# Graph attention: constant rows added by matmuls over 128 partitions instead of 4

## The chip, the cores and the metric

The kernel runs on one core of one Trainium2 chip. The metric is the device time of one execution in microseconds (us), taken as the median of several runs. Of this kernel, changes of under 0.2% (about 6.4 us) can hardly be told from no change.

## The reference, cut to what matters

A conditioned transformer layer (`L0`) is followed by a graph attention layer (`L1`) over the same rows. There are 2 batches of 2048 rows with 512 features each, 16 heads of 32, and 20 graph nodes (the first rows of each batch) that every row attends to, in two directions.

```python
def reference(x, cond, mask, ...):
    x = L0(x, cond, ...)                 # adaptive norm, attention, adaptive norm, MLP
    v, q, adj_f = x, cond, mask.astype(float32)
    row_zero = v.sum(-1) == 0
    q_exp = where(row_zero[..., None], 0.0, q[:, None, :])
    self_feat = concatenate([v, q_exp], -1) @ W_self.T + b_self
    output = self_feat
    for d in range(2):
        A = (adj_f if d == 0 else swapaxes(adj_f, 1, 2))[:, :, :20, :]
        cond_adj, vb = A.sum(-1), A @ w_bias + b_bias
        kv = self_feat[:, :20]
        qh, kh = heads(self_feat @ Wq[d].T + bq[d]), heads(kv @ Wk[d].T + bk[d])
        aff = einsum('bnhd,bmhd->bnhm', qh, kh) / sqrt(32)
        w = softmax(where(cond_adj[:, :, None] > 0, aff, -9e15) + vb[:, :, None])
        output = output + out_heads(w, kv, Wout[d]) + bout[d]
    return v + relu(output)
```

For a row `x` of the graph layer, both the scores of all heads and the `self_feat` part are linear in `x`, plus a part that depends only on whether the row's sum is zero (then the condition vector drops out), plus constants. These last two parts are what the change is about.

## The kernel before, in words

The kernel is one program in which each engine has its own instruction list, written out by hand; semaphores order the lists against each other. The stages are: projections, attention, output projection, feed-forward (eight chunks of 512 rows, 16 slices of the hidden layer each), a shared stage that folds the graph weights, and the graph stage over 32 tiles of 128 rows.

TensorE (`pe` in the code, PE in the profile; its weight loads are PEld) does each matmul as a weight load, up to 128 rows by 128 columns, and a stream of up to 512 columns through these weights. Most operands are rounded float32 (`F32R`) in high and low halves, three products for one.

In the graph stage a tile `t` takes these steps on TensorE, in this order of lines in the profile:

- `pe_score(t + 1)`: 24 matmuls of 320 columns at L1728 (two directions into two PSUM banks), then two at L1732 that add the constant rows: the weights are `nzT`, four rows by 128 columns, and the stream is `rows`, four rows by 320 columns.
- `pe_turn_w(t)`: six transposes at L1753 of the softmax weights `ex`; `pe_turn_x(t + 2)`: four transposes at L1711 of the next rows.
- `pe_self(t + 1)`: 12 matmuls of 512 columns at L1741, then one at L1743 that adds the constant rows of this part, four rows again.
- `pe_turn_nz(t + 2)`: one transpose at L1718 that turns `nzt` (128 rows by 4 columns: twice "the row's sum isn't zero", twice 1) into PSUM, from where ScalarE copies it into `nzT` (L1803).
- `pe_heads(t)`: six products at L1762, in 12 matmuls, of the turned weights `wT` with `vw`.

Beside it VectorE adds the edge bias (L1877), takes maxima, sums and reciprocals of the softmax and writes the output (L1898); GpSimd (POOL) subtracts the maximum (L1928) and multiplies by the reciprocal (L1931); ScalarE does the exponential and copies.

`rows` has four rows for each batch: the condition's part in high and low half, and the constant part in high and low half. They are written once by VectorE in `dve_rows` (L1341), twice in the last feed-forward chunk and four times in the shared stage. `pool_graph_start(1)` fills four tiles with zeros in the last feed-forward chunk (L1424 to L1427). `pool_graph` fills `nzt` with ones before the tiles (L1922).

Of the kernel before, what the change touches and what calls it, by code (L numbers as in the profile page):

```python
# [7 lines left out]
F32 = mybir.dt.float32  # L8
F32R = mybir.dt.float32r
I32 = mybir.dt.int32  # L10
ALU = mybir.AluOpType
ACT = mybir.ActivationFunctionType
AX = mybir.AxisListType

B, S, D = 2, 2048, 512
# [163 lines left out]
def program(nc, a):  # L179
    pe, act, dve, pool, sp = nc.tensor, nc.scalar, nc.vector, nc.gpsimd, nc.sync  # L180
# [14 lines left out]
    with ExitStack() as ctx:  # L195
        cursor = [(nc.sbuf_base + 31) // 32 * 32]

        def sem(name):
            return ctx.enter_context(nc.semaphore(name))

        def place(name, shape, at, dt=F32):
            return nc.alloc_sbuf_tensor_at(name, list(shape), dt, offset=at)

        def take(name, shape, dt=F32):
            at = cursor[0]
            cursor[0] += (4 * int(np.prod(shape[1:])) + 31) // 32 * 32
            return place(name, shape, at, dt)

        ps = ctx.enter_context(nc.psum_tensor("ps", [128, 8, 512], F32))
# [926 lines left out]
        def early(name, *shape, dt=F32):  # L1136
            n = (4 * int(np.prod(shape[1:])) + 31) // 32 * 32
            if spot[0] < spots[0][1] < spot[0] + n:
                spot[0] = spots[0][1]
            at = spot[0]  # L1140
            spot[0] += n
            at = spots[0][0] + at if at < spots[0][1] else spots[1][0] + at - spots[0][1]
            return place(name, shape, at, dt)[(slice(None),) * len(shape)]

        rt = early("rt", 4, 2, D)
        rows = early("rows", 4, B, D + 640, dt=F32R)
        brow, bm = early("brow", 3, D), early("bm", 120, 96)
        wbB, m4, sel, onb = early("wbB", 128, 12), early("m4", 128, 4), early("sel", 4, 2), early("onb", 3, 4)
        colb, condT2 = early("colb", 128, 5, NK), early("condT2", 128, NK, B)
# [8 lines left out]
               (0, 1): place("gm01", [128, NK, 320], at1 + 54272), (1, 1): place("gm11", [128, NK, 320], at1 + 59392)}  # L1158
        s_cw_wc, s_cw_wv, s_cw_k0, s_cw_q0, s_cw_k1, s_cw_q1, s_cw_nat, s_cw_o0 = s_qst
        n_cw = 32 * NC8 + 16  # L1160
        s_cw_o1, s_small, s_x40 = sem("s_cw_o1"), sem("s_small"), sem("s_x40")
        (s_xT, s_xTc, s_nz, s_nzm, s_nzb, s_prep, s_qt, s_qtc, s_kvm, s_kv, s_rowm, s_rhi,
         s_rlo, s_khm, s_kh, s_gmm, s_gma, s_gmd, s_ggm, s_ggh, s_ggl, s_vwm, s_vw, s_wvh, s_wvl) = (
            sem(n) for n in ("s_xT", "s_xTc", "s_nz", "s_nzm", "s_nzb", "s_prep",
# [168 lines left out]
        def dve_rows(i, b, bank, c0, w):  # L1333

            hi, lo = rt[:, 0, 0:w], rt[:, 1, 0:w]
            dve.wait_ge(s_rhi, i + 1)
            dve.tensor_tensor(lo, ps[0:4, bank, 0:w], hi, ALU.subtract).then_inc(s_rlo, 1)
            dve.wait_ge(s_rlo, 3 * i + 1)
            dve.tensor_scalar(lo, lo, sel[:, 1:2], None, ALU.mult).then_inc(s_rlo, 1)
            dve.wait_ge(s_rlo, 3 * i + 2)  # L1340
            dve.scalar_tensor_tensor(out=rows[:, b, c0:c0 + w], in0=hi, scalar=sel[:, 0:1], in1=lo, op0=ALU.mult,  # L1341
                                     op1=ALU.add).then_inc(s_rlo, 1)

        def dve_kh(d, bank):
# [76 lines left out]
        def pool_graph_start(f):  # L1421

            if f == 1:
                pool.memset(lc[:, :, :, 2:4], 0.0).then_inc(s_prep, 1)  # L1424
                pool.memset(lq, 0.0).then_inc(s_prep, 1)
                pool.memset(lb[:, :, :, 0:2], 0.0).then_inc(s_prep, 1)
                pool.memset(kvr.rearrange("p d b k h e n -> p (d b k h e n)"), 0.0).then_inc(s_prep, 1)  # L1427
            elif f == 2:
                pool.wait_ge(s_small, 16 * NSMALL)
                pool.tensor_copy(lc[:, :, :, 0:2], condT2.rearrange("p k b -> p b k").unsqueeze(3)  # L1430
                                 .to_broadcast([128, B, NK, 2])).then_inc(s_prep, 1)
                pool.tensor_copy(lb[:, :, :, 2:4], colb[:, 1:3, :].unsqueeze(3)
                                 .to_broadcast([128, 2, NK, 2])).then_inc(s_prep, 1)
            elif f == 6:
                kvT4 = kvT.rearrange("p k (b n) -> p k b n", b=B)
                pool.wait_ge(s_kv, 3)
                pool.wait_ge(s_prep, 4)
                for b in range(B):
                    for d in range(2):
                        pool.tensor_copy(kvr[:, d, b, :, :, d, :], kvT4[:, :, b, :].unsqueeze(2)  # L1440
                                         .to_broadcast([128, NK, 3, NG])).then_inc(s_prep, 1)
                pool.tensor_copy(lq[:, :, :, 0:2], qtT.rearrange("p k b -> p b k").unsqueeze(3)
                                 .to_broadcast([128, B, NK, 2])).then_inc(s_prep, 1)
                pool.wait_ge(s_prep, 11)
                for b in range(B):
                    pool.tensor_copy(lq[:, b, :, 2:4], colb[:, 0, :].unsqueeze(2)
                                     .to_broadcast([128, NK, 2])).then_inc(s_prep, 1)
# [79 lines left out]
        def ff_over(eng):  # L1527

            eng.wait_ge(s_f1, NQ)
            eng.wait_ge(s_f2, 4 * NQ)  # L1530
            eng.wait_ge(s_ro, 4 * NC8)
# [132 lines left out]
        rc = take("rc", [128, 2, 32])  # L1664
        tsum = take("tsum", [128, 2])
        nzt = take("nzt", [128, 2, 4])
        nzT = take("nzT", [4, 2, 128], F32R)
        s_xt, n_xt = s_x3, [(NT - 1 - i) // 5 + 1 for i in range(5)]
        s_ad, n_ad = s_a3, [(NT - 1 - i) // 3 + 1 for i in range(3)]
        s_st, n_st = s_x2, [(NT - 1 - i) // 5 + 1 for i in range(5)]  # L1670
# [6 lines left out]
        def weights_read(eng):  # L1677

            eng.wait_ge(s_gmm, 16)
            for t in range(4):  # L1680
                eng.wait_ge(s_rs[t], 16 * (n_rs + NC8))
# [117 lines left out]
        def act_turn_nz(t):  # L1799
            act.wait_ge(s_tz, t + 1)  # L1800
            if t >= 2:
                act.wait_ge(s_self, t - 1)
            act.activation(nzT[:, t % 2, :], ps[0:4, 7, 0:128], ACT.Copy).then_inc(s_zT, 1)  # L1803

        def act_turn_w(t):
            for r0, q0, q1 in ((120, 0, 3), (120, 3, 4), (80, 4, 6)):
# [27 lines left out]
        def dve_zero(t):  # L1834
            j = t % 2
            dve.wait_ge(s_zs, t + 1)
            dve.wait_ge(s_nz1, 1)
            if t >= 2:
                dve.wait_ge(s_tz, t - 1)
            dve.tensor_scalar(nzt[:, j, 0:2], tsum[:, j:j + 1].to_broadcast([128, 2]), 0.0, None,  # L1840
                              ALU.not_equal).then_inc(s_nzv, 1)
# [77 lines left out]
        def pool_graph():  # L1919
            ff_over(pool)  # L1920
            weights_read(pool)
            pool.memset(nzt[:, :, :], 1.0).then_inc(s_nz1, 1)  # L1922
            pool.wait_ge(s_wvl, 1)
            for t in range(NT):
                j = t % 2
                a3, e3 = groups(af[:, j, :]), groups(ex[:, j, :])
                pool.wait_ge(s_mx, t + 1)
                pool.tensor_tensor(a3, a3, mx[:, j, :].unsqueeze(2).to_broadcast([128, 32, NG]),  # L1928
                                   ALU.subtract).then_inc(s_sub, 1)
                pool.wait_ge(s_rc, t + 1)  # L1930
                pool.tensor_tensor(e3, e3, rc[:, j, :].unsqueeze(2).to_broadcast([128, 32, NG]),  # L1931
                                   ALU.mult).then_inc(s_w, 1)
# [83 lines left out]
```

## Time and profile before

| what | us |
|---|---|
| median of 3 runs (3178.0 to 3180.33) | 3179.2 |
| the profiled execution | 3179.57 |
| its span, first to last instruction | 3178.2 |
| TensorE busy in the span | 3132.2 (99%) |
| VectorE busy | 2153.4 (68%) |
| GpSimd busy | 1539.2 (48%) |
| ScalarE busy | 1388.3 (44%) |

The profiled execution is 0.37 us above the median of the runs, and its span is 1.37 us shorter than its time. The graph stage, from the first transposes at 2848 us to the end, is 330 us of the span. In the profile, `4*128` in a matmul's row means weights of four rows by 128 columns; the shape behind it is that of the stream. A matmul's length includes its way through the array, so successive matmuls overlap in the record; the distance between two starts tells how long one holds the engine. Idle time "issue" means that the profile shows nothing that the engine waited for.

### The profile page before, as it was taken

The page shows a single profiled execution, that of the slowest core. Times are in us where ns is not written, and L with a number is a line of the kernel's source. Part 1 is how long each engine was busy: PE and PEld are TensorE (multiplying, and loading weights), DVE is VectorE, ACT ScalarE, POOL GpSimd, SP SyncE. Part 2 cuts the span into 40 slices and gives each one's busy share as a digit, 9 for nine tenths or more (in the row PEclk, how much of TensorE's full clock was granted, in tenths as well). Part 3 has the DMA queues.
Part 4 walks back from the last instruction along what each step waited for, and adds up shares of the span by engine and source line. Part 5 has one row for each costly group of instructions (what it writes and reads, how often), then busy time and mean ns, then how long its engine had stood idle before and what let it go on. Part 6 is the DMA issues. An engine that isn't in the chain of part 4 may idle for free.

```text
span 3178.2 us, 43496 instructions
## 1 busy us (share of the span) xinstructions
PE 3132.2 (99%) x16394; PEld 2171.5 (68%) x16394; DVE 2153.4 (68%) x3633; ACT 1388.3 (44%) x2703; POOL 1539.2 (48%) x654
## 2 busy tenths in 40 slices
PE   8999999999999999999999998999999999999999
PEld 7887655555555555555555546788888887878888
DVE  4557889999999999998998966433333332236666
ACT  2221467666666667666666652311111111113232
POOL 0000488988889889889889854100000001002222
PEclk9999999999999999999999999999999999899999
DMA  6674777978888887878878667311110013112221
GB/s 203 189 234 143 179 166 166 199 151 182 181 174 172 174 184 161 194 169 169 193 153 185 141 167 266 123 40 40 40 40 27 14 40 107 55 32 67 77 77 55
DMA packets 169367, 423.43 MB, mean 133 GB/s; under 512 B 18492, under 2 KB 60604, under 8 KB 141863
## 3 DMA queue, kind: packets, MB, share of 16 engines
q0 software_dynamic: 27744, 201.08, 31.2%
q1 hardware_dynamic: 139639, 214.07, 22.3%
q10 hardware_dynamic: 1776, 5.51, 0.7%
q8 instruction: 130, 2.13, 0.3%
q14 instruction: 78, 0.64, 0.1%
HBM read 143.51 MB, written 75.50 MB: 69 GB/s over the span
## 4 chain that ended last, share of the span: by engine, by line
PE 94%; DVE 2%; DMA 2%; issue 1%; POOL 1%; ACT 1%; SPq 0%; DVEq 0%; ACTq 0%; POOLq 0%
PE ps L384 16%; PE ps L672 15%; PE ps L683 15%; PE ps L1194 11%; PE ps L1181 11%; PE ps L460 5%; PE ps L1728 4%; PE ps L464 3%; PE ps L1741 3%; PE ps L689 2%; PE ps L1762 1%; PE ps L1557 1%; PE ps L1045 1%; DMA ao<-ao_d 1%; PE ps L158 1%; PE ps L1753 1%
## 5 line engine op out<-in xcount | busy, mean ns | idle before, releaser
L397 DVE TENSOR_REDUCE nmp<-ps 128x1 f32<-128x512 f32 x1966 | 1200.1, 681 | 108.2 <-PE ps L384 103.8
L762 ACT ACTIVATE pt<-ps 128x512 f32<-128x512 f32 x2048 | 1030.9, 628 | 458.1 <-PE ps L672 454.8
L861 POOL TENSOR_TENSOR pt<-pt 128x2048 f32<-128x2048 f32 x217 | 995.6, 4588 | 120.2 <-ACT pt L762 114.7
L672 PE MATMUL ps<-qs,ks 128*128 128x512 f32 x2048 | 811.2, 400 | 2.5 <-ACT pt L762 2.5
L384 PE MATMUL ps<-ks,qs 96*128 96x512 f32 x1966 | 804.5, 409 | 0.1
L384 PEld LDWEIGHTS ps<-ks,qs 96*128 96x128 f32 x1966 | 373.3, 190 | 264.5 <-DVE nmp L397 167.0
L683 PE MATMUL ps<-pt,vq 128*32 128x512 f32 x4096 | 492.5, 599 | 0.0
L672 PEld LDWEIGHTS ps<-qs,ks 128*128 128x128 f32 x2048 | 389.9, 191 | 95.5 <-ACT pt L762 18.9
L1181 PE MATMUL ps<-hpb,w 128*128 128x512 f32 x1536 | 384.0, 400 | 3.4 <-DMA x_d<-x 3.4
L1194 PE MATMUL ps<-w,gp 128*128 128x512 f32 x1536 | 379.0, 396 | 1.3 <-DVE gp L1330 1.3
L1181 PEld LDWEIGHTS ps<-hpb,w 128*128 128x128 f32 x1536 | 291.0, 191 | 69.8 <-issue 5.6
L1194 PEld LDWEIGHTS ps<-w,gp 128*128 128x128 f32 x1536 | 288.9, 188 | 69.8 <-DVE gp L1330 1.7
L1328 DVE CAST gp<-g 128x512 fp32r<-128x512 f32 x128 | 60.9, 476 | 400.6 <-ACT g L1317 400.6
L1317 ACT ACTIVATE g<-ps,b1c 128x512 f32<-128x512 f32 x128 | 88.1, 688 | 530.1 <-PE ps L1181 530.1
L1455 POOL TENSOR_TENSOR res<-res,b2B 128x512 f32<-128x512 f32 x32 | 41.3, 1318 | 491.0 <-DMA res<-x_d 491.0
L683 PEld LDWEIGHTS ps<-pt,vq 128*32 128x32 f32 x4096 | 107.2, 109 | 244.7 <-ACT pt L762 163.0
L139 POOL TENSOR_SCALAR ve<-mv 128x4 f32<-128x4 f32 x16 | 4.0, 250 | 383.1 <-DVE mv L134 383.1
L853 POOL DMA_DIRECT2D pt<-pt x189 | 165.8, 877 | 42.3 <-PE ps L683 36.8
L866 POOL TENSOR_TENSOR pt<-pt 128x2048 f32<-128x2048 f32 x31 | 142.6, 4601 | 7.8 <-DMA pt<-pt 3.2
L493 ACT ACTIVATE st<-ps,bqk 128x512 fp32r<-128x512 f32 x64 | 43.8, 688 | 227.1 <-PE ps L460 223.3
L1928 POOL TENSOR_TENSOR af<-af,mx 128x640 f32<-128x640 f32 x32 | 40.8, 1275 | 191.1 <-DVE mx L1883 191.1
L1728 PE MATMUL ps<-gg,xp 128*128 128x320 f32 x768 | 122.7, 317 | 0.0
(169 smaller groups left out, 3020.1 us busy)
## 6 DMA issues: line engine op xcount, KB each, us to landing
pt<-pt POOLq DMA_DIRECT2D x189, 1024.0 KB, 8.5
qk_d<-st SPq DMA_DIRECT2D x128, 256.0 KB, 2.9
qs<-qk_d SPq DMA_DIRECT2D x87, 256.0 KB, 4.8
ks<-qk_d SPq DMA_DIRECT2D x42, 512.0 KB, 8.3
xina<-in_x SPq DMA_DIRECT2D x8, 1024.0 KB, 6.5
v_d<-vst SPq DMA_DIRECT2D x32, 256.0 KB, 2.6
vq<-v_d SPq DMA_DIRECT2D x32, 256.0 KB, 4.3
ao_d<-accs SPq DMA_DIRECT2D x32, 256.0 KB, 6.8
```

Source lines behind the costliest of these rows:

```text
L384: pe.matmul(ps[:, ring.bank["max", u], :], qsb[0:96, v % 3, hq // 4, 128 * (hq % 4):128 * (hq % 4) + 128], ksb[w % 2][0:96, hq // 4, CH * ...
L397: dve.tensor_reduce(nmp[:, n // 4, n % 4:n % 4 + 1], ps[:, ring.bank["max", u], :], AX.X, ALU.max, negate=True).then_inc(s_mr, 1)
L460: m = pe.matmul(ps[:, bank, :], w[:, x, k, col:col + 128], hp[:, y, k, :], start=(i == 0 and k == 0), stop=(i == 2 and k == NK - 1))
L672: pe.matmul(ps[:, score_bank(n), :], ksb[w % 2][:, hh, 128 * kt:128 * kt + 128], qsb[:, v % 3, hh, :], start=True, stop=True).then_inc(s_s ...
L683: m = pe.matmul(ps[32 * hh:32 * hh + 32, 7, :], vq[:, kt, 32 * hh:32 * hh + 32], pt[:, exp_slot(g), hh, :], start=(kt == 0), stop=(kt == 15))
L762: act.activation(pt[:, exp_slot(g), hh, :], ps[:, score_bank(n), :], ACT.Exp, scale=SCALE).then_inc(s_exp, 1)
L853: pool.dma_start(accumulator(v, 1 + d), pt[:, exp_slot(g), :, :], accum_op=ALU.add).then_inc(s_dma[d], 16)
L861: pool.tensor_tensor(accumulator(v, 0), accumulator(v, 0), pt[:, exp_slot(g), :, :], ALU.add).then_inc(s_add, 1)
L866: pool.tensor_tensor(accumulator(v, 0), accumulator(v, 0), accumulator(v, 2), ALU.add).then_inc(s_add, 1)
L1181: m = pe.matmul(ps[:, 4 + r, :], w1[:, f // 4, x, k, 128 * (f % 4):128 * (f % 4) + 128], hp[:, y, k, :], start=(i == 0 and k == 0), stop=( ...
L1194: m = pe.matmul(ps[:, t, :], gp[:, q % 2, x, 128 * t:128 * t + 128], w2[:, f // 4, y, f % 4, :], start=(i == 0 and f == 0), stop=(i == 2 a ...
L1728: pe.matmul(ps[:, 1 + d, 0:320], xp[:, j, x, 128 * k:128 * k + 128], gg[b][:, y, k, 320 * d:320 * d + 320], start=(i == 0 and k == 0), sto ...
```

## The change

`rows` and `nzT` get 128 partitions instead of 4. The four live rows stay in partitions 0 to 3; GpSimd fills both tiles with zeros beforehand, and VectorE (through the new semaphore `s_rz` and one more count of `s_nz1`) waits for these fills before it writes into `rows`, and before the first `nzt`. The matmuls at L1732 and L1743 use all of both tiles. The bytes that a tile takes in a partition are the same.

```diff
-        rows = early("rows", 4, B, D + 640, dt=F32R)
+        rows = early("rows", 128, B, D + 640, dt=F32R)
...
+            dve.wait_ge(s_rz, 1)
+            dve.scalar_tensor_tensor(out=rows[0:4, b, c0:c0 + w], in0=hi, scalar=sel[:, 0:1], in1=lo, op0=ALU.mult,
...
             if f == 1:
+                pool.memset(rows.rearrange("p b n -> p (b n)").bitcast(F32), 0.0).then_inc(s_rz, 1)
                 pool.memset(lc[:, :, :, 2:4], 0.0).then_inc(s_prep, 1)
...
-        nzT = take("nzT", [4, 2, 128], F32R)
+        nzT = take("nzT", [128, 2, 128], F32R)
...
-            act.activation(nzT[:, t % 2, :], ps[0:4, 7, 0:128], ACT.Copy).then_inc(s_zT, 1)
+            act.activation(nzT[0:4, t % 2, :], ps[0:4, 7, 0:128], ACT.Copy).then_inc(s_zT, 1)
...
-            dve.wait_ge(s_nz1, 1)
+            dve.wait_ge(s_nz1, 2)
...
             weights_read(pool)
+            pool.memset(nzT[:, :, :].rearrange("p t n -> p (t n)").bitcast(F32), 0.0).then_inc(s_nz1, 1)
             pool.memset(nzt[:, :, :], 1.0).then_inc(s_nz1, 1)
```

TensorE's, ScalarE's and SyncE's lists keep their order; each matmul stands where it stood. GpSimd's list gets two rows. Before, in the last feed-forward chunk and up to the first tile of the graph stage (`kvr`, `lc`, `lq`, `lb` are operands of the shared stage):

```order
547 L1424 MEMSET lc 128x8x2 [waits s_lo]
548 L1425 MEMSET lq 128x32
549 L1426 MEMSET lb 128x8x2
550 L1427 MEMSET kvr 128x1920
551 L1430 COPY lc<-condT_120 128x8x2 [waits s_small]
```

After, at the same place, then at the start of the graph stage:

```order
547 L1425 MEMSET rows 128x2304 [waits s_lo]
548 L1426 MEMSET lc 128x8x2
549 L1427 MEMSET lq 128x32
550 L1428 MEMSET lb 128x8x2
551 L1429 MEMSET kvr 128x1920
552 L1432 COPY lc<-condT_120 128x8x2 [waits s_small]
...
559 L1924 MEMSET nzT 128x256 [waits s_vst0,s_vst1,s_gmm,s_vst2,s_ro,s_vst3,s_f2,s_f1]
560 L1925 MEMSET nzt 128x8
561 L1931 TENSOR_TENSOR af<-af,mx 128x640 [waits s_mx,s_wvl]
```

The fill of `rows` now stands ahead of the four older fills, and the fill of `nzT` ahead of that of `nzt`; what follows on GpSimd comes in the same order as before. Line numbers behind the new lines move by one to three.

## Rows read from the trace of the kernel before

**Rows 1.** Busy time by stretch: stretch, PE, PEld, DVE, ACT, POOL busy, granted clock, DMA

```profile
2900.00:2950.00 50.00, 50.00 (x312) 42.81 (x310) 34.90 (x67) 15.17 (x41) 12.74 (x10) 1.00 0.23 76
```

**Rows 2.** Chain of waits, 2780 to the end: start, length, what

```profile
2945.72 0.48 PE ps L1732 x2
...
3165.43 0.50 PE ps L1732 x2
...
3175.43 0.69 DVE ot L1898
```

**Rows 3.** TensorE, 2940.16 to 2940.72: start, length, what, rows*columns of its weights, shape

```profile
2939.85 0.39 PE L1741 MATMUL ps<-wvp,xp 128*128 128x512 f32 x1
2940.17 0.50 PE L1743 MATMUL ps<-rows,nzT 4*128 4x512 f32 x1
2940.60 0.27 PE L1718 MATMUL ps<-ident,nzt 128*4 128x128 f32 x1
```

**Rows 4.** TensorE inside a run of L1741

```profile
2939.16 1.08 PE L1741 MATMUL ps<-wvp,xp 128*128 128x512 f32 x4
```

**Rows 5.** TensorE around L1732's two matmuls, from four windows in order of time

```profile
2944.98 0.75 PE L1728 MATMUL ps<-gg,xp 128*128 128x320 f32 x4
...
2945.42 0.31 PE L1728 MATMUL ps<-gg,xp 128*128 128x320 f32 x1
2945.66 0.41 PE L1732 MATMUL ps<-rows,nzT 4*128 4x320 f32 x1
...
2945.91 0.30 PE L1732 MATMUL ps<-rows,nzT 4*128 4x320 f32 x1
...
2946.14 0.87 PE L1753 MATMUL ps<-ident,ex 128*120 128x128 f32 x6
2946.85 0.60 PE L1711 MATMUL ps<-ident,xt 128*128 128x128 f32 x4
```

**Rows 6.** Line L1743: its weight loads (ns min/median/max), and idle before them (us, times)

```profile
L1743 PEld LDWEIGHTS ps<-rows,nzT x32: 181/182/182, 2861.6 to 3169.4; 4*128 4x128 f32 x32
...
  issue: 11.4, 32
```

**Rows 7.** Line L1728: weight loads of all 128 rows (ns min/median/max)

```profile
L1728 PEld LDWEIGHTS ps<-gg,xp x768: 187/188/337, 2852.1 to 3165.0; 128*128 128x128 f32 x192
```

**Rows 8.** TensorE elsewhere: a full-row transpose right behind 512-column matmuls

```profile
2590.86 0.40 PE L1194 MATMUL ps<-w,gp 128*128 128x512 f32 x1
2591.09 0.27 PE L158 MATMUL ps<-ident,xinb 128*128 128x128 f32 x1
```

**Rows 9.** TensorE elsewhere: a matmul with four weight columns behind 512-column matmuls

```profile
2696.41 0.40 PE L1194 MATMUL ps<-w,gp 128*128 128x512 f32 x1
2696.73 0.59 PE L1251 MATMUL ps<-wcT,lc 128*4 128x512 f32 x1
```

**Rows 10.** TensorE at the first tile: the four-column transpose behind L1711

```profile
2848.32 0.66 PE L1711 MATMUL ps<-ident,xt 128*128 128x128 f32 x4 [0.31 <-DVE vw L1640]
2848.81 0.27 PE L1718 MATMUL ps<-ident,nzt 128*4 128x128 f32 x1
```

**Rows 11.** In order of time: last feed-forward chunk, then GpSimd's fill in the shared stage

```profile
2657.73 1.70 POOL L1427 MEMSET kvr<- 128x1920 f32 x1
...
2658.87 0.84 DVE L1328 CAST gp<-g 128x512 fp32r<-128x512 f32 x1 [3.49 <-ACT g L1317]
...
2663.54 2.96 PE L1194 MATMUL ps<-w,gp 128*128 128x512 f32 x12
...
2781.62 0.10 POOL L1922 MEMSET nzt<- 128x8 f32 x1 [90.15 <-PE ps L1211]
```

**Rows 12.** Line L1840 on VectorE (ns min/median/max)

```profile
L1840 DVE TENSOR_SCALAR nzt<-tsum x32: 159/1089/1093, 2848.3 to 3158.0; 128x2 f32<-128x2 f32 x32
```

**Rows 13.** GpSimd and TensorE one tile on, in order of time

```profile
2953.14 1.28 POOL L1931 TENSOR_TENSOR ex<-ex,rc 128x640 f32<-128x640 f32 x1 [3.80 <-DVE rc L1892]
...
2956.13 0.87 PE L1753 MATMUL ps<-ident,ex 128*120 128x128 f32 x6
```

More of the change, by code:

```diff
@@ L1160, in program @@
         n_cw = 32 * NC8 + 16
-        s_cw_o1, s_small, s_x40 = sem("s_cw_o1"), sem("s_small"), sem("s_x40")
+        s_cw_o1, s_small, s_x40, s_rz = sem("s_cw_o1"), sem("s_small"), sem("s_x40"), sem("s_rz")
         (s_xT, s_xTc, s_nz, s_nzm, s_nzb, s_prep, s_qt, s_qtc, s_kvm, s_kv, s_rowm, s_rhi,
@@ L1340, in dve_rows @@
             dve.wait_ge(s_rlo, 3 * i + 2)
-            dve.scalar_tensor_tensor(out=rows[:, b, c0:c0 + w], in0=hi, scalar=sel[:, 0:1], in1=lo, op0=ALU.mult,
+            dve.wait_ge(s_rz, 1)
+            dve.scalar_tensor_tensor(out=rows[0:4, b, c0:c0 + w], in0=hi, scalar=sel[:, 0:1], in1=lo, op0=ALU.mult,
                                      op1=ALU.add).then_inc(s_rlo, 1)
```

## The prediction

> **What bounds the kernel now.** I read the busy time by stretch first. In the graph stage TensorE is busy for all of the 50 us that are shown, at a granted clock of 1.00 (the upper level, 2.4 GHz), while VectorE has 34.9, GpSimd 12.7 and ScalarE 15.2 us of work [rows 1]. The chain of waits says the same: tile after tile it runs through TensorE alone, and leaves it only behind the last L1732 at 3165.43, for a tail through the other engines that ends with the last output at 3175.43 + 0.69 us [rows 2]. So whatever holds TensorE in a tile counts 30 times, once a lap of 2956.13 - 2946.14 = 9.99 us [rows 5, 13].
>
> Then I read TensorE's starts in order of time, since successive matmuls overlap in the record and only distances between starts tell what one costs. A plain L1741 of 512 columns takes (1.08 - 0.39) / 3 = 0.23 us to the next start [rows 4]; a plain L1728 of 320 columns (0.75 - 0.31) / 3 = 0.147; a plain transpose L1711 (0.60 - 0.27) / 3 = 0.11 [rows 5]. The four-row matmuls cost more on both of their sides, though they stream no more columns. L1741 to L1743 takes 0.32 us, and L1743 to the next start 0.43, both against 0.23 [rows 3]. L1728 to the first L1732 takes 0.24, the first to the second 0.25, the second to L1753 0.23, all against 0.147, and the six L1753 that follow have (0.87 - 0.27) = 0.60 us between their first and last start instead of 5 x 0.11 = 0.55 [rows 5].
>
> Why they cost more shows in the weight loads. The load for L1743 is preceded by 11.4 us of idle time in 32 times, 0.36 us each, and ends it for no reason that the profile has a name for [rows 6]. No semaphore stands ahead of L1743, so this isn't data that came late. A full 128-row load takes 0.188 us [rows 7], more than the 0.147 from one L1728 to the next, so full-row loads do lie beside the stream before them. The four-row load of 0.182 us doesn't: engine and weights are emptied before it, and again before the full-row load after it.
>
> **The change part by part.** L1743 and L1732 become matmuls of the very form of L1741 and L1728: the same rows, columns, type and stream length. I take their distances as the plain ones. What each place gives back in a tile:
>
> - ahead of L1743: 0.32 - 0.23 = 0.09 us
> - behind L1743: 0.43 - 0.23 = 0.20 us
> - ahead of the first L1732: 0.24 - 0.147 = 0.093 us
> - between the two: 0.25 - 0.147 = 0.103 us
> - behind the second: 0.23 - 0.147 = 0.083 us
> - in the L1753 behind it: 0.60 - 0.55 = 0.05 us
>
> Together 0.62 us of the lap of 9.99. The counts differ. The tail begins at the last L1732, so the two at L1743 count for 31 tiles, those up to the second L1732 for 32, those behind it for the 30 tiles in which L1753 follows and which aren't the last. The sum is 31 x 0.29 + 32 x 0.196 + 30 x 0.133 = 8.99 + 6.27 + 3.99 = 19.25 us. Each distance is rounded to 0.01 us, so this can be off by some 2 us.
>
> The 0.20 is the term to doubt, because what follows L1743 is L1718, a transpose with weights of only four columns. Two rows bound it. A full transpose behind a 512-column matmul starts after 2591.09 - 2590.86 = 0.23 us, no penalty [rows 8]. An ordinary matmul with four weight columns starts after 2696.73 - 2696.41 = 0.32 us, 0.09 more [rows 9]. L1718 itself is seen behind L1711 once at the upper clock: the last of the four L1711 starts at 2848.32 + 0.66 - 0.27 = 2848.71, and L1718 0.10 later, the plain distance of transposes [rows 10]. A transpose with four columns pays nothing there, so I take 0.23 and keep 0.32 as the other end. The Trainium skill (TensorEngine Tiling, Overview and Tiling Modes) has small column counts run in a narrower tiling mode and the engine drained whenever the mode changes; by this L1718 would keep a drain and the sum be 16.5. Its restrictions (Tile-to-Partition Mapping) say that column tiling goes without transposes of fp32 input; by this L1718 runs in the full array, and the sum stays 19.25. The row of L1718 agrees with the second.
>
> The new 128-row loads take 0.188 us instead of 0.182 [rows 6, 7] and lie beside the stream ahead of them, as those of L1728 do. If that cover were gone, each would stand in the open, and the result is the rival of no gain, below.
>
> The fills are GpSimd's. That of `rows` is estimated from the 128x1920 fill: 1.70 x 2304 / 1920 = 2.04 us [rows 11]. It goes ahead of this fill in the last feed-forward chunk, so the work queued behind it, four fills and some copies, comes about 2 us later. GpSimd's work and VectorE's can collide: the cast L1328 beside that fill took 0.84 us [rows 11], and L1840 takes 0.159 us alone but 1.09 as its usual case, while GpSimd is at L1928 [rows 12]. If both fills held the cast to their end, it would begin at 2657.73 + 1.70 + 2.04 = 2661.47, be over by 2662.31 and leave 1.23 us for L1330, which works on a tile of the same size (0.84 us, by estimate, at the length of that cast), before TensorE's next L1194 at 2663.54 [rows 11]. So a cover of about 0.4 us is left in the worst case; I cost the fill at nothing, and at 1 us if the cover is gone. VectorE needs `s_rz` first behind slice 7 of the chunk, and the fill is issued by slice 2; a slice is 24 matmuls of 0.23 us, 5.5 us, so there are over 25 us between. The fill of `nzT`, 1.70 x 256 / 1920 = 0.23 us, stands ahead of the fill of `nzt` at 2781.62 [rows 11], which VectorE's first L1840 needs at 2848.3 [rows 12]: 66 us of cover. Each `dve_rows` now waits for one more semaphore, which has long been raised. Nothing else moves.
>
> What is late next: the softmax chain from L1732 over VectorE, GpSimd, ScalarE and back to L1753. It begins at the second L1732, 2945.91 [rows 5], GpSimd's L1931 ends at 2953.14 + 1.28 = 2954.42, and TensorE takes it up at 2956.13 [rows 13]: 1.71 us to spare. A lap shorter by 0.62 leaves 1.09. VectorE has 34.9 / 50 x 9.99 = 7.0 us of work in a lap [rows 1] that will be 9.37. So TensorE stays the bound.
>
> **The sum** is 3179.57 - 19.25 = 3160.3 us for the profiled execution, which is 0.37 above the median of the runs; for the median I predict 3160.0 us, 0.6% less.
>
> **The rivals.**
>
> *The transpose keeps its stall.* 0.09 x 31 = 2.8 us less of a gain: 3162.8 us. For it speaks the 0.32 of rows 9, against it the 0.10 of rows 10. Chance 10%.
>
> *The rows are not what costs.* The gaps could belong to these accumulating matmuls, to their tiles or to their place, and stay with 128 rows: 3179.2 us, as before. For it: in the graph stage no matmul but these two has four rows, so rows and place aren't told apart there. Against it: loads of the same columns and type are beside the stream everywhere else. The Trainium skill (TensorE: Matmul & The Clock Gate, "Why this matters for your kernels") says that a single matmul of 32 rows takes as long as one of 128, and (Part 3) that a load passes a running matmul only where it goes to other rows of the array; by these rules filling up rows gains nothing. The loads of rows 7, longer than the distance between their matmuls, don't agree with the second. Chance 6%.
>
> *Only a part comes.* If one of the two lines keeps its stalls, the gain is 8.99 or 10.26 us: 3170.2 or 3168.9 us. Nothing in the rows speaks for that. Chance 2%.
>
> *Slower: the shorter lap sets GpSimd against VectorE.* Each collision such as L1840's adds 1.09 - 0.16 = 0.93 us [rows 12] to the chain that ends at L1753. Up to 1.71 us it costs no more than the gain; beyond this the lap is longer than before. Three new collisions are 2.79 us, 1.08 over the point: 30 x 1.08 = 32 us, 3212 us. Against it: almost all of the chain hangs on L1732 itself and moves with it as a whole, and only L1898, which waits for L1762, shifts within it. Chance 2%.
>
> **How the numbers follow.** The forecast has 80%. Its own spread is the rounding (2 us) and that of the runs (1.2 us): 3157 to 3163. The range reaches over the transpose's case with the same spread, 3157 to 3166, and leaves out the rest. Faster by more than 0.2%, below 3172.8, are the forecast, the transpose's case and the partial one: 92%. Within 0.2%, which is what a measurement here can't tell from no change: 6%. Slower: 2%.
>
> **What would show it.** In the profile after, L1732 and L1743 should read `128*128`; L1741 to L1743 and L1743 to L1718 should take 0.23 us, the four distances at L1732 0.147; the idle time "issue" ahead of the loads of L1732 and L1743 should be gone and that ahead of L1753 too; the lap should be 9.37 us, and VectorE's wait ahead of L1877 shorter by 0.6. An L1718 at 0.32 shows the transpose's case. Idle time of TensorE ahead of L1753 with GpSimd as its releaser, in mid-stage, shows the last rival. Distances of 0.32 and 0.43 with 128 rows would make the prediction wrong at its root.

## The result: 3156.7 us, 0.7% faster, and the profile after

| what | before | after |
|---|---|---|
| median of 6 runs each, us | 3178.6 (3169.32 to 3184.61) | 3156.66 (3143.74 to 3160.59) |
| ratio after/before, 95% interval | | 0.9929 [0.9905, 0.9952] |
| the profiled execution, us | 3179.57 | 3160.59 |
| lap of the graph stage, start to start of the 24 score matmuls, median, us | 9.987 | 9.327 |

The kernel got faster by the mechanism that was predicted. The time lies 3.3 us under the forecast of 3160.0 and 0.34 us under the low end of its range. In the profile of after the line numbers of the graph stage are two to three higher (L1728, L1732, L1741, L1743, L1718, L1753 became L1730, L1734, L1743, L1745, L1720, L1755).

The first part of the page of after, the busy time of each engine in the span:

```profile
span 3159.2 us, 43504 instructions
...
PE 3110.9 (98%) x16394; PEld 2172.3 (69%) x16394; DVE 2157.3 (68%) x3633; ACT 1388.7 (44%) x2703; POOL 1542.9 (49%) x656
```

TensorE lost 21.3 us of the 3132.2 before, and the span 19.0. VectorE and GpSimd gained 4 us each, which cost nothing. Where the time came from shows in the weight loads. This is L1745 of after, the line that was L1743 [rows 6], with its weight loads (ns min/median/max, first and last start):

```profile
L1745 PEld LDWEIGHTS ps<-rows,nzT x32: 187/188/188, 2862.9 to 3150.2; 128*128 128x128 f32 x32
```

There is no row "issue" any more: the 11.4 us of idle time that no semaphore explained are gone. From the first load to the last it is 287.3 us; in [rows 6] it was 307.8. These 20.5 us, over 31 laps, are the change. The span lost 1.5 us less: in this profile the first transposes of the graph stage start 3.2 us later, at 2851.51 us against 2848.32 in [rows 10], and 1.7 of them were made good ahead of the first and behind the last of these loads.

One lap of after in order of time, from four windows (start, length, what), to be held against [rows 3, 5, 13]:

```profile
2950.73 0.31 PE L1730 MATMUL ps<-gg,xp 128*128 128x320 f32 x1
2950.88 0.46 PE L1734 MATMUL ps<-rows,nzT 128*128 128x320 f32 x2
...
2951.18 0.82 PE L1755 MATMUL ps<-ident,ex 128*120 128x128 f32 x6
2951.38 0.89 DVE L1879 TENSOR_TENSOR af<-ps,c 128x320 f32<-128x320 f32 x2 [1.96 <-PE ps L1734]
...
2953.27 1.23 DVE L1842 TENSOR_SCALAR nzt<-tsum 128x2 f32<-128x2 f32 x1
...
2954.79 0.39 PE L1743 MATMUL ps<-wvp,xp 128*128 128x512 f32 x1
2955.02 0.39 PE L1745 MATMUL ps<-rows,nzT 128*128 128x512 f32 x1
2955.24 0.27 PE L1720 MATMUL ps<-ident,nzt 128*4 128x128 f32 x1
...
2958.27 1.28 POOL L1934 TENSOR_TENSOR ex<-ex,rc 128x640 f32<-128x640 f32 x1 [3.80 <-DVE rc L1894]
...
2960.50 0.82 PE L1755 MATMUL ps<-ident,ex 128*120 128x128 f32 x6
```

Read the distances of starts. L1743 to L1745 takes 0.23 us, where [rows 3] had 0.32; L1745 to the transpose L1720 0.22, where it was 0.43. L1730 to the first L1734 takes 0.15, the two L1734 are 0.46 - 0.31 = 0.15 apart, and the second is 0.15 ahead of L1755; in [rows 5] these were 0.24, 0.25 and 0.23. The six L1755 lie 0.82 - 0.27 = 0.55 apart, no longer 0.60. The lap is 2960.50 - 2951.18 = 9.32 us, that of [rows 5, 13] 9.99. GpSimd's L1934 ends at 2959.55, 0.95 us ahead of the L1755 that needs it: the softmax chain became tighter by 0.76 us, and still doesn't bound. TensorE is as full as in [rows 1], with more in the same stretch:

```profile
2900.00:2950.00 50.00, 50.00 (x336) 46.76 (x336) 38.25 (x72) 15.11 (x40) 13.83 (x11) 1.00 0.23 76
```

It issues 336 matmuls in 50 us instead of 312. That VectorE went from 34.9 to 38.25 us is mostly more laps in the stretch (34.9 x 9.987 / 9.327 = 37.4). The rest fits L1842, the L1840 of [rows 12]: it takes 1.23 us a lap now instead of 1.09, off the path.

The fills held up VectorE longer than GpSimd's fills did before, and still cost nothing. GpSimd, VectorE and TensorE of after in the last feed-forward chunk, then GpSimd's fill in the shared stage (the engines' other rows between these are left out):

```profile
2662.06 2.02 POOL L1425 MEMSET rows<- 128x2304 f32 x1
...
2663.70 2.44 DVE L1328 CAST gp<-g 128x512 fp32r<-128x512 f32 x1 [3.49 <-ACT g L1317]
...
2664.17 1.69 POOL L1429 MEMSET kvr<- 128x1920 f32 x1
2665.82 0.38 POOL L1432 COPY lc<-condT 128x16 f32<-128x16 f32 x1
...
2666.18 0.70 DVE L1330 TENSOR_TENSOR gp<-g,gp 128x512 fp32r<-128x512 f32 x1
2668.37 2.96 PE L1194 MATMUL ps<-w,gp 128*128 128x512 f32 x12
2669.29 0.43 DVE L1328 CAST gp<-g 128x512 fp32r<-128x512 f32 x1 [2.42 <-ACT g L1317]
...
2786.14 0.31 POOL L1924 MEMSET nzT<- 128x256 f32 x1 [90.22 <-PE ps L1211]
```

The cast began in the fill of `rows` and ended at 2666.14, when GpSimd was done with both long fills and about done with the copy behind them: 2.44 us, against 0.84 in [rows 11] and 0.43 for the next cast, which has no fill beside it. L1330 was done at 2666.88, and TensorE's next L1194 came at 2668.37: 1.5 us to spare.

### The profile page after: what moved, and what is told of

Read it like the earlier page. It is cut to its first block, busy times and chain, and to the rows that moved or that the text cites. A ratio compares the mean times of both kernels' runs of the same rounds, so it can differ in the third digit from the quotient of the medians.

```text
span 3159.2 us, 43504 instructions
## 1 busy us (share of the span) xinstructions
PE 3110.9 (98%) x16394; PEld 2172.3 (69%) x16394; DVE 2157.3 (68%) x3633; ACT 1388.7 (44%) x2703; POOL 1542.9 (49%) x656
## 4 chain that ended last, share of the span: by engine, by line
PE 94%; DVE 2%; DMA 2%; issue 1%; POOL 1%; ACT 1%; SPq 0%; DVEq 0%; ACTq 0%; POOLq 0%
PE ps L384 16%; PE ps L672 15%; PE ps L683 15%; PE ps L1194 11%; PE ps L1181 11%; PE ps L460 5%; PE ps L1730 4%; PE ps L464 3%; PE ps L1743 3%; PE ps L689 2%; PE ps L1764 1%; PE ps L1559 1%; PE ps L1045 1%; DMA ao<-ao_d 1%; PE ps L158 1%
## 5 line engine op out<-in xcount | busy, mean ns | idle before, releaser
L672 PE MATMUL ps<-qs,ks 128*128 128x512 f32 x2048 | 810.5, 399 | 2.5 <-ACT pt L762 2.5
L672 PEld LDWEIGHTS ps<-qs,ks 128*128 128x128 f32 x2048 | 389.1, 190 | 95.4 <-ACT pt L762 18.9
L1181 PE MATMUL ps<-hpb,w 128*128 128x512 f32 x1536 | 381.9, 398 | 3.4 <-DMA x_d<-x 3.4
L1194 PE MATMUL ps<-w,gp 128*128 128x512 f32 x1536 | 380.4, 396 | 2.1 <-DVE gp L1330 2.1
L1194 PEld LDWEIGHTS ps<-w,gp 128*128 128x128 f32 x1536 | 289.4, 188 | 71.4 <-DVE gp L1330 2.5
L1181 PEld LDWEIGHTS ps<-hpb,w 128*128 128x128 f32 x1536 | 289.0, 190 | 69.8 <-issue 5.6
L1730 PE MATMUL ps<-gg,xp 128*128 128x320 f32 x768 | 121.7, 315 | 0.0
```

Source lines behind the costliest of these rows:

```text
L672: pe.matmul(ps[:, score_bank(n), :], ksb[w % 2][:, hh, 128 * kt:128 * kt + 128], qsb[:, v % 3, hh, :], start=True, stop=True).then_inc(s_s ...
L1181: m = pe.matmul(ps[:, 4 + r, :], w1[:, f // 4, x, k, 128 * (f % 4):128 * (f % 4) + 128], hp[:, y, k, :], start=(i == 0 and k == 0), stop=( ...
L1194: m = pe.matmul(ps[:, t, :], gp[:, q % 2, x, 128 * t:128 * t + 128], w2[:, f // 4, y, f % 4, :], start=(i == 0 and f == 0), stop=(i == 2 a ...
L1730: pe.matmul(ps[:, 1 + d, 0:320], xp[:, j, x, 128 * k:128 * k + 128], gg[b][:, y, k, 320 * d:320 * d + 320], start=(i == 0 and k == 0), sto ...
```

## The experiments

The lap below is the median distance, over the whole graph stage, from the start of one tile's score matmuls to that of the next; it repeats to some ns between profiles, while the medians of runs move by several us (a part of the reason is shown further down). No kernel here leaves any of the computation out. Where no median of several runs is given, the kernel ran once.

**The fills alone.** After, with both matmuls reading four rows again.

```diff
-                pe.matmul(ps[:, 1 + d, 0:320], nzT[:, j, :], rows[:, b, D + 320 * d:D + 320 * d + 320],
+                pe.matmul(ps[:, 1 + d, 0:320], nzT[0:4, j, :], rows[0:4, b, D + 320 * d:D + 320 * d + 320],
...
-            pe.matmul(ps[:, 3 + j, :], nzT[:, j, :], rows[:, b, 0:D], start=False, stop=False,
+            pe.matmul(ps[:, 3 + j, :], nzT[0:4, j, :], rows[0:4, b, 0:D], start=False, stop=False,
```

> Both tiles have 128 partitions and both fills run, but the matmuls at L1734 and L1745 read partitions 0 to 3 only. Theory A (what costs is that a matmul with four rows stands between matmuls with 128: the engine empties on both sides): a lap of 9.99 us as in the kernel before, starts 0.32 and 0.43 us apart around L1745, a median within 3 us of the kernel before. Theory B (the place of the tiles, or the wait for the fills, brought the gain): a lap near 9.33 us and about 20 us less than before. If the fills cost something it shows here alone, as up to 1 us more.

Measured: 3182.41 us, ratio to before 0.9999 [0.9984, 1.0014], lap 9.987. Its L1745:

```profile
L1745 PEld LDWEIGHTS ps<-rows,nzT x32: 181/181/181, 2863.9 to 3171.7; 4*128 4x128 f32 x32
...
  issue: 11.4, 32
```

The idle time is back to the digit. So the larger tiles, the fills and the added waits leave the lap as it was and change the time by nothing that these runs can tell; the gain is in the rows that the matmuls read.

**One line each.** After, with L1745 alone on four rows (the score part is kept), and with L1734 alone on four rows (the self part is kept): one of the two edits above each.

> L1734 reads 128 partitions, L1745 only 0 to 3. Theory A with independent places: a lap of 9.99 - 0.093 - 0.103 - 0.083 - 0.05 = 9.66 us, about 10.3 us less than before. Theory C (one four-row matmul in a lap is enough to hold the engine, so either half alone brings little): a lap over 9.8 us. The starts at L1745 keep 0.32 and 0.43 us.

> L1745 reads 128 partitions, L1734 only 0 to 3. Theory A: a lap of 9.99 - 0.09 - 0.20 = 9.70 us by rounded starts, about 9 us less than before. If the pace inside L1743 (0.232 us before, 0.227 at its end after) is also set by L1745, the lap is 9.65 us. Theory C: over 9.8 us.

Measured, score part: lap 9.640, 0.347 less than before; 3166.65 us, 0.9957 [0.9941, 0.9972]. Self part: lap 9.693, 0.294 less; 3174.79 us, 0.9975 [0.9964, 0.9986]. Each line pays for itself, and the two together (0.641) make 0.660 but for 0.02. This 0.02 is in the pace of the 12 full-row matmuls of `pe_self` (L1743, before L1741): the eleven distances between their starts, by the medians over the laps, sum to 2.636 us in the kernel before and with the self part, 2.628 with the score part, and 2.607 with both. L1745 with the score part, then with the self part:

```profile
L1745 PEld LDWEIGHTS ps<-rows,nzT x32: 181/181/182, 2849.3 to 3146.3; 4*128 4x128 f32 x32
```

```profile
L1745 PEld LDWEIGHTS ps<-rows,nzT x32: 187/188/188, 2862.0 to 3160.5; 128*128 128x128 f32 x32
```

From the first load to the last these are 297.0 and 298.5 us, 10.8 and 9.3 less than the 307.8 of [rows 6]. By the laps the parts are worth 31 x 0.347 = 10.8 and 31 x 0.294 = 9.1 us; by the medians, 16.0 and 7.9 (before in the same call: 3182.65). The medians aren't good enough to divide 20 us into two parts; that of the score part rests on four runs, one of them 10 us below the next. That run is the profiled one, and it is taken up below.

**After once more,** the same kernel beside those three.

> The changed kernel once more, for the size. Theory A: the laps give 31 x 0.66 = 20.5 us, so a ratio of 0.9935 with an interval that holds it, and single runs spread over some 10 us because of stages before the graph stage. Theory D (the change also gains elsewhere, such as in the feed-forward or the shared stage): a ratio below 0.992 and a shorter stretch before the first transposes of the graph stage than the 2848.3 us of before, beyond what single profiles differ by.

Measured: 3158.72 us (3153.59 to 3165.31), 0.9927 [0.9914, 0.994], lap 9.327 again. The two medians of after are 2 us apart.

**How many rows.** After, with both matmuls on 64, 65 or 33 rows of the same tiles:

```diff
...
-            pe.matmul(ps[:, 3 + j, :], nzT[:, j, :], rows[:, b, 0:D], start=False, stop=False,
+            pe.matmul(ps[:, 3 + j, :], nzT[0:64, j, :], rows[0:64, b, 0:D], start=False, stop=False,
...
```

> The matmuls at L1734 and L1745 read partitions 0 to 63, zeros from 4 on. Theory A1 (the array is split by rows in steps, and up to 64 rows go into a split array, which must be emptied before and after): a lap of 9.99 us, 0.32 and 0.43 us around L1745 as with four rows. Theory A2 (cost falls with every row added): 60 of 124 rows added, a lap of about 9.67 us. Theory A3 (only very few rows cost): 9.33 us.

> As before this with partitions 0 to 64. Theory A1: 65 rows no longer fit the half array and run as full ones, so a lap of 9.33 us, 0.227 us on both sides of L1745. Theory A2: 9.66 us, next to that of 64 rows. If only a full set of 128 rows is free of the stall: 9.99 us.

> As before this with partitions 0 to 32. Theory A1: a split array again, 9.99 us. Theory A2: 9.83 us. Theory A3: 9.33 us.

Measured: 64 rows 3181.96 us, lap 9.98; 65 rows 3158.16 us, lap 9.353; 33 rows 3187.49 us, lap 9.98 (before in that call: 3182.22). L1745 with 64 rows, with 65, and with 33, one fence each:

```profile
L1745 PEld LDWEIGHTS ps<-rows,nzT x32: 182/183/183, 2863.2 to 3170.9; 64*128 64x128 f32 x32
...
  issue: 11.3, 32
```

```profile
L1745 PEld LDWEIGHTS ps<-rows,nzT x32: 187/188/188, 2858.4 to 3146.5; 65*128 65x128 f32 x32
```

```profile
L1745 PEld LDWEIGHTS ps<-rows,nzT x32: 182/183/183, 2869.2 to 3176.8; 33*128 33x128 f32 x32
...
  issue: 11.3, 32
```

One row more, from 64 to 65, takes the whole stall away, and the load's time steps with it from 183 to 188 ns; 33 and 64 rows stall just as four do. So it isn't a cost that grows or shrinks with the rows, but a state with a border between 64 and 65. The Trainium skill (TensorEngine Tiling (Array Packing), Tiling Modes) has 32-row, 64-row and 128-row modes, and an engine that is drained when the mode changes. The traces agree with a border behind 64 rows, with a lap of 9.98 us on the one side and 9.353 on the other; of the drain they show the idle time ahead of the loads, 11.3 us or none, and between 4 and 33 rows they show no border. That a matmul changes sides by its rows alone, with nothing else in the program changed, is this measurement's.

**Four-row matmuls side by side.** Before, with the four-row matmul of the self part moved right behind the two of the score part, so that the tile leaves the full-row work once instead of twice. It opens the sum in its bank instead of closing it, and waits for the bank.

```diff
+            if t >= 2:
+                pe.wait_ge(s_out, t - 1)
+            pe.matmul(ps[:, 3 + j, :], nzT[:, j, :], rows[:, b, 0:D], start=True, stop=False, skip_group_check=True)
...
-                              start=(i == 0 and k == 0), stop=False, skip_group_check=True)
-            pe.matmul(ps[:, 3 + j, :], nzT[:, j, :], rows[:, b, 0:D], start=False, stop=False,
-                      skip_group_check=True).then_inc(s_self, 1)
...
+                              start=False, stop=False, skip_group_check=True)
+            m.then_inc(s_self, 1)
```

> The kernel before, with four rows; but the four-row matmul of the self part is issued right behind the two at L1732, opens its PSUM bank, and the 12 of L1741 add to it. Theory A (the array is emptied where the row mode changes): two changes of mode in a lap instead of four. The 0.09 ahead of the matmul goes, of the 0.20 behind it about 0.1 goes (the emptying) and 0.1 stays (its load in the open, as between the two L1732): a lap of 9.80 us, about 6 us less than before. Theory E (each four-row matmul has a price of its own wherever it stands): a lap of 9.99 us and no difference.

Measured: 3172.4 us, 0.9973 [0.9957, 0.9989], lap 9.70. TensorE of it at the place, in order of time:

```profile
2910.29 0.56 PE L1732 MATMUL ps<-rows,nzT 4*128 4x320 f32 x2
2910.69 0.39 PE L1736 MATMUL ps<-rows,nzT 4*128 4x512 f32 x1
2911.01 0.32 PE L1755 MATMUL ps<-ident,ex 128*120 128x128 f32 x1
```

The second L1732 starts at 2910.29 + 0.25 = 2910.54 and L1736 0.15 behind it: among four-row matmuls the plain distance holds, and the load doesn't stand in the open. The 0.32 behind L1736 is one return to full rows. So the price is one for each change between few rows and full rows, not one for each four-row matmul. The 0.25 between the two L1732 belongs to the change as well: it is the second start after it, and the third, L1736, is on time.

**One change more.** Before, with the self part's matmul cut into two of 256 columns, the first among the 12 full-row ones.

```diff
+                    if (i, k) == (1, 1):
+                        pe.matmul(ps[:, 3 + j, 0:256], nzT[:, j, :], rows[:, b, 0:256], start=False, stop=False,
+                                  skip_group_check=True)
-            pe.matmul(ps[:, 3 + j, :], nzT[:, j, :], rows[:, b, 0:D], start=False, stop=False,
+            pe.matmul(ps[:, 3 + j, 256:512], nzT[:, j, :], rows[:, b, 256:512], start=False, stop=False,
```

> The kernel before, with the four-row matmul L1743 cut into two of 256 columns: one behind the sixth of the 12 matmuls of L1741, one where it stood. The same columns are streamed, but a lap has six changes between four-row and full-row weights instead of four. Theory A (the change of mode is paid, whatever is streamed): the 0.09 ahead and the 0.20 behind are paid once more, a lap of 9.99 + 0.29 = 10.28 us, some 9 us more than before. Theory E (the four-row stream itself is slow, by the column): a lap of 9.99 us.

Measured: 3193.95 us (before 3181.42), lap 10.387, 0.400 more. TensorE at the place:

```profile
2911.81 1.32 PE L1741 MATMUL ps<-wvp,xp 128*128 128x512 f32 x5
2913.05 0.38 PE L1744 MATMUL ps<-rows,nzT 4*128 4x256 f32 x1
2913.36 0.50 PE L1741 MATMUL ps<-wvp,xp 128*128 128x512 f32 x1
```

The last of the five L1741 starts at 2911.81 + 1.32 - 0.39 = 2912.74, L1744 0.31 later, and the next L1741 0.31 behind that. With the same columns streamed in all, one more time out of the full rows and back costs 0.40 us a lap. Both distances of 0.31 are a part of it, and by the medians of the starts the second L1741 after the return comes 0.337 us behind the first, where the same place takes 0.231 in the kernel before. So the return makes two starts late here. Behind L1718 it doesn't: L1762 follows it after 0.108 us before as after (L1764 behind L1720). Read like this, the 0.43 behind L1743 in [rows 3] holds two late starts at once, the second after the way in and the first after the way out; that reading wasn't tested by itself.

**The same for columns.** In the shared stage of after, two kinds of matmul have weights of four columns. Here they get 68 (the further ones zero or unused).

```diff
-        lc, lq, lb = early("lc", 128, B, NK, 4), early("lq", 128, B, NK, 4), early("lb", 128, 2, NK, 4)
+        lc, lqb = early("lc", 128, B, NK, 4), early("lqb", 128, 2, NK, 72)
+        lq, lb = lqb[:, :, :, 0:68], lqb[:, :, :, 4:72]
...
-                pe.matmul(ps[0:4, i, 0:320], lq[:, b, k, :], gm_[d, b][:, k, :], start=(k == 0), stop=False,
+                pe.matmul(ps[0:68, i, 0:320], lq[:, b, k, :], gm_[d, b][:, k, :], start=(k == 0), stop=False,
```

> The changed kernel, and in the shared stage the weights of the two matmul groups with four columns (lq and lb) are widened to 68 columns with zeros, or in four of them with other rows' values that nobody reads. Theory A for columns (over 64 columns the array is not split): L1559 to L1568 takes 0.269 us instead of 0.362, L1571 to L1600 0.07 instead of 0.162, and the next one 0.105 instead of 0.180: 4 x 0.26 = 1.0 us less in the shared stage, too little for the median, which stays within 3 us of the changed kernel's. If narrow columns are not what costs there: 0.362 and 0.162 as before.

Measured: 3158.6 us, 0.992 [0.9894, 0.9946], lap 9.327. The first of these matmuls in after, and then here:

```profile
2794.68 0.70 PE L1559 MATMUL ps<-gm,wnat 128*128 128x320 f32 x2
2795.31 0.43 PE L1568 MATMUL ps<-gm,lq 128*4 128x320 f32 x1
```

```profile
2792.97 0.43 PE L1562 MATMUL ps<-gm,wnat 128*128 128x320 f32 x1
2793.24 0.43 PE L1571 MATMUL ps<-gm,lqb 128*68 128x320 f32 x1
```

With four columns the distance is 2795.31 - (2794.68 + 0.70 - 0.43) = 0.36 us, with 68 it is 0.27, and so it is in all four places of the stage: narrow weights among full ones pay the 0.09 of [rows 9] too. It happens too seldom here to be seen in the time of the kernel.

**The clock in the shared stage.** Why did one run of the score part take 10 us less than the next? TensorE of before in the shared stage, and the stretch around it (busy time of PE, PEld, DVE, ACT, POOL; granted clock; DMA), each in a fence of its own, and then the same two views of that run:

```profile
2757.57 3.74 PE L1203 MATMUL ps<-kvT,wkT 128*128 128x40 f32 x32 [0.94 <-PE ps L1194]
2761.13 20.20 PE L1211 MATMUL ps<-khb,wqn 128*128 128x80 f32 x96
```

```profile
2760.00:2785.00 25.00, 25.00 (x116) 23.63 (x116) 5.44 (x10) 4.42 (x7) 0.10 (x1) 0.53 0.10 30
```

```profile
2758.33 3.74 PE L1203 MATMUL ps<-kvT,wkT 128*128 128x40 f32 x32 [0.94 <-PE ps L1194]
2761.89 10.92 PE L1211 MATMUL ps<-khb,wqn 128*128 128x80 f32 x96
```

```profile
2760.00:2785.00 25.00, 25.00 (x170) 20.59 (x170) 8.38 (x15) 6.56 (x12) 0.35 (x2) 1.00 0.21 70
```

The same 96 matmuls take 20.20 us at the lower level of the clock (1.2 GHz) and 10.92 us at the upper one (2.4 GHz): 9.3 us between two executions, on lines that the change doesn't touch. In after they take:

```profile
2765.10 20.75 PE L1211 MATMUL ps<-khb,wqn 128*128 128x80 f32 x96
```

Of the profiles with these 80 columns, eleven have 19.9 to 20.8 us here, and this one 10.92. What goes ahead of the fall is L1203, 32 matmuls of 40 columns, each behind a load of 128 rows; the same 32, in the same 3.74 us, go ahead in the score part's run, in which no fall follows, and why is not shown. To see whether the fall hangs on how short the streams are, the last experiment but one doubles the columns of the 96 (160 in three of four, the further 80 overwritten by the next matmul):

```diff
+            kf = khb[:, d, b, :, :].rearrange("p g n -> p (g n)")
...
-                m = pe.matmul(ps[:, bank, 80 * g:80 * g + 80], wqn[d][:, g, 128 * kin:128 * kin + 128],
-                              khb[:, d, b, g, :], start=True, stop=True)
+                n = 160 if g < NK - 1 else 80
+                m = pe.matmul(ps[:, bank, 80 * g:80 * g + n], wqn[d][:, g, 128 * kin:128 * kin + 128],
+                              kf[:, 80 * g:80 * g + n], start=True, stop=True)
```

> On the spread of the runs, which the range of the prediction missed. The changed kernel; the matmuls of pe_gm at L1211 stream 160 columns instead of 80 in three of four (the second half is overwritten by the next one, the outputs are unchanged). In the kernel before and in the changed one the 96 of the shared stage take 20.2 us at the half clock; in the profile of score_only they took 10.9 us at the full clock. Theory H (the clock falls there because short streams behind long loads leave the array little to do): with fuller streams the clock holds, the 96 take about 72 x 0.134 + 24 x 0.112 = 12.3 us, the stretch from the last L1194 to the first L1559 shrinks from 25 to about 17 us, and the median is some 8 us under the changed kernel's, with a smaller spread. Theory I (what comes ahead, L1203 and the wait there, sets the clock for this stretch): the clock is at half all the same, the 96 take 72 x 0.267 + 24 x 0.213 = 24.3 us, and the median is 4 us over the changed kernel's.

Measured: 3151.19 us (four runs), 0.9913 [0.9897, 0.993]. The 96 matmuls, and the stretch:

```profile
2768.54 14.33 PE L1213 MATMUL ps<-khb,wqn 128*128 128x160 f32 x96
```

```profile
2760.00:2785.00 25.00, 24.06 (x155) 22.32 (x154) 7.29 (x14) 4.27 (x7) 0.35 (x2) 0.93 0.14 51
```

With twice the columns they take 14.33 us, six less: some 14 of them run at the lower level (0.267 us from start to start), the rest at the upper one (0.136). So the clock falls in this profile too, and is back earlier than in the eleven with 80 columns. Both of the last two edits at once:

> The changed kernel with the edits of wide_cols and of gm160 together. Theory A with H: they touch different matmuls and add up, 1.0 us from the wide columns (or 0.9, by what wide_cols showed) and the fuller streams' 14.3 us instead of 20.2 for the 96 matmuls; the median lies 6 to 9 us under the changed kernel's, a ratio of 0.990 to 0.992 to the kernel before. Rival: the clock's gain in gm160 was one of its ordinary good runs, and the ratio is that of the changed kernel, 0.9928.

Measured: 3155.04 us (3151.12 to 3159.5), 0.9923 [0.9904, 0.9942]; the 96 matmuls take 14.78 us:

```profile
2767.83 14.78 PE L1214 MATMUL ps<-khb,wqn 128*128 128x160 f32 x96
```

The interval holds that of after in its second call (0.9914 to 0.994). The 6 us are in both profiles, but the runs don't separate these kernels from after; that they are faster isn't shown.

## Why the prediction was right, and where it went wrong

- **What bounds** was right: TensorE was full before and is full after, and what a tile lost came out of the lap whole. In each experiment with several runs a shorter lap came with a shorter time, of 0.9 to 1.5 times what the laps say where nothing else was changed.
- **The six places** came as worked out. Before they made 0.32 + 0.43 + 0.24 + 0.25 + 0.23 + 0.60 = 2.07 us, after 0.23 + 0.22 + 0.15 + 0.15 + 0.15 + 0.55 = 1.45, a difference of 0.62. By the medians over all laps it is 0.625. But the lap fell by 0.660, and the gain over the laps is 20.5 us where the sum had 19.25. Most of what the sum lacks is no rounding: it is the pace of the 12 L1743 themselves, 2.636 us before and 2.607 after for their eleven distances. The prediction put it at nothing, since it took only the two sides of the four-row matmuls; it is 0.029 us a lap, 0.9 of the missing 1.2 us. Why the pace depends on the rows of other matmuls is open.
- **The load in the open** didn't hold as a reason. The prediction says that a four-row load doesn't lie beside the stream ahead of it. Among four-row matmuls it does: the third one (L1736 above) starts 0.15 us behind the second. So the 0.25 between the two L1732 is a price of the change from full rows, not of each four-row load. The sum isn't touched by this, since with 128 rows both prices are gone.
- **The term to doubt**, the transpose with four columns, was chosen rightly: it starts 0.22 us behind L1745. Narrow weights do pay 0.09 in ordinary matmuls (0.36 against 0.27 above), and in this transpose they don't. So the rival by which the transpose keeps its stall is excluded.
- **The rows, not the place:** the rival by which the gaps belong to these matmuls or their place fell with the fills alone (lap 9.987) and with 64 and 65 rows (9.98 and 9.353). The rival that only a part comes fell with the two kernels of one line each.
- **The fills:** 2.02 us against 2.04, 0.31 against 0.23. The worst case for the cast came (it went on through both fills, to 2666.14), yet 1.5 us of cover were left, not 0.4: the cast ended 0.28 us behind the last long fill, where the prediction had it begin there and take 0.84 us, and the fill of `rows` began 1.64 us ahead of the cast, not 1.14 as `kvr`'s in [rows 11]. They cost nothing, as put, by the fills alone (0.9999).
- **The slower rival:** VectorE's wait ahead of its first step fell from 2.69 to 2.01 us a tile, 0.68 where 0.6 was named, and GpSimd still ends 0.95 us ahead of TensorE's need (1.09 was forecast). No collision reached the path. The sums over 32 tiles, of before and of after, from the line of that step:

```profile
  PE ps L1732: 86.0, 32
```

```profile
  PE ps L1734: 64.3, 32
```

**The step that failed** is "Its own spread is the rounding (2 us) and that of the runs (1.2 us)". The mechanism held, and the size of the spread didn't. It was read off three runs within 2.3 us. Over all calls before ran from 3164.93 to 3188.12, after from 3143.74 to 3165.31: more than 20 us each, as much as the change is worth.

A good part is the granted clock in the shared stage, 9.3 us between two profiles. The runs' mean clocks speak for it: of the 19 runs of before beside the first four kernels, the four at 0.991 to 0.993 took 3169.3 to 3177.0 us, the nine at 0.987 and 0.988 took 3182.5 to 3188.1; the fastest of before in all (3164.93) had 0.994, the fastest of after (3143.74) 0.993. That the shared stage at the upper level is what makes such a run was seen in one trace (the score part's, 0.994), and for the others it stays an inference. Another part arises ahead of that stage: the last L1194 in front of it starts at 2756.2 us in the profile of before and at 2765.1 in that with 33 rows. Most of these 8.9 us lie between the last L672 of the attention and the first L1181 of the feed-forward, 117.8 us in the one and 125.3 in the other (granted clock 0.99 and 0.95); what makes this stretch differ isn't settled. In the trace of before the low clock was to be seen: 0.53 in 25 us of a span that has 0.989 in all. Here such a stretch went otherwise in another run, and the range should have reached some 10 us below the forecast on its account.

Of the 3.3 us between forecast and median, the sum accounts for 1.2 (the pace of L1743 above all), and 0.6 lie in the start: before had a median of 3178.6 beside after, and the prediction began from 3179.2. The other 1.5 are less than the 2 us between the two medians of after. So that the time came out just below the range, by 0.34 us, is as much chance as a fault of the sum.

Some of the expectations recorded with the experiments missed as well. With the four-row matmuls side by side 9.80 us was expected, with the load between them in the open, and 9.70 came: that is 9.987 less the whole 0.29 of the self part, so one change in and out goes entirely. For the cut matmul 10.28 was expected, by the price of one place, and 10.387 came: among 512-column matmuls the second start after the return is late too. With 160 columns the 96 matmuls were to take 12.3 us, if the clock held, or 24.3, if it was low for all of them; 14.33 came, between the two. With both edits 6 to 9 us less than after was expected, a ratio of 0.990 to 0.992, and 0.9923 came.

## What to carry to other kernels

Going over to matmuls of 64 rows or fewer among full-row ones, and back, costs 0.29 to 0.40 us here, with streams of 256 to 512 columns; fill their operands up with zeros to more than 64 rows if their tiles have the partitions to spare, or put all such matmuls of a tile side by side, so that the engine changes over once. Look for it where weight loads have idle time that no semaphore explains. And before a range is set from a few runs, look in the trace for stretches at half clock: here one of them was where another run differed by 9 us.

## What the runs showed of the hardware that wasn't expected

- The border lies between 64 and 65 rows, with nothing between: the lap is 9.98 us with 33 or 64 rows and 9.353 with 65 (9.987 with four, 9.327 with 128).
- Among few-row matmuls the plain distance holds (0.15 us), and the weight load of 183 ns hides beside the stream ahead of it as full-row loads do.
- A change can make two starts late, not one: 0.24 and 0.25 us on the way to four rows, then 0.15; on the way back to 512-column matmuls 0.31, then 0.337 against 0.231 us. Behind the transpose L1718 the second start is on time (0.108 us).
- Columns have the like, 0.09 us for four columns among 128 and none for 68, but not in a transpose of four columns (0.22 us behind L1745).
- A VectorE cast of 0.43 us took 2.44 us beside GpSimd's fills and ended 0.28 us behind the last long one. The Trainium skill (SBUF — State Buffer, "SBUF: two separate sides") has the two engines share a port pair that one of them holds for a whole instruction. This row agrees in kind, though the cast waited through several of GpSimd's instructions.
